# Soft mixture-of-experts in a perceiver block: combine gates turned as plain exponentials and normalised on VectorE as they leave PSUM

## What is computed

```
logits = (x @ phi_w.T + phi_b).reshape(t, z, n=64 experts, p=32 slots)
D = softmax(logits, axis=slots)        # dispatch weights
C = softmax(logits, axis=experts)      # combine weights (the gates)
X_tilde = einsum('tznp,tzd->npd', D, x)
X_tilde = clip(X_tilde, -33000, 65000)
X_tilde = tanh((X_tilde - mean) * rsqrt(var + 1e-5))
Y_tilde = einsum('npd,ndH->npH', X_tilde, expert_w) + expert_b
out = x + einsum('tznp,npH->tzH', C, Y_tilde)
```

## Time and profile before

| | us |
|---|---|
| median of 3 runs | 644.53 (641.23 to 645.74) |
| the profiled execution's own time | 640.95 |
| its span in the profile | 639.2 |

### The profile page before, as it was taken

The page is one execution under the profiler, slowest core; times in us unless marked ns, Lnnn a source line. Parts: engine busy times, 40 slices in busy tenths (PEclk is TensorE's granted clock), DMA queues, the critical chain, the costliest instruction groups (busy, mean ns, idle before and its releaser), DMA issues. The chain is left out here.

```text
span 639.2 us, 10389 instructions
## 1 busy us (share of the span) xinstructions
PE 583.5 (91%) x3740; PEld 469.4 (73%) x3740; DVE 406.8 (64%) x798; ACT 337.5 (53%) x988; POOL 255.0 (40%) x209
## 2 busy tenths in 40 slices
PE   5998999999999999998797789899999993699998
PEld 4887999899989999987565566455556882577787
DVE  3756565756665667644777586788889986733100
ACT  2545454434544446752787585259889953343210
POOL 1353153313241325124479464223455867643000
PEclk9999999999999999999999699999999998799999
DMA  7223121212110220067057500400000925359000
GB/s 267 71 99 116 35 67 67 84 49 84 67 67 34 71 88 26 3 193 203 1 155 199 175 1 1 133 1 0 1 1 19 180 67 197 102 179 300 31 26 25
DMA packets 39688, 55.62 MB, mean 87 GB/s; under 512 B 3923, under 2 KB 34515, under 8 KB 38870
## 3 DMA queue, kind: packets, MB, share of 16 engines
q1 hardware_dynamic: 39638, 54.97, 28.4%
HBM read 47.60 MB, written 7.35 MB: 86 GB/s over the span
## 5 line engine op out<-in xcount | busy, mean ns | idle before, releaser
L382 POOL TENSOR_TENSOR ctx_lo<-front,ctx_hi 128x1024 fp32r<-128x1024 f32 x32 | 76.4, 2389 | 155.7 <-DVE ctx_hi L824 135.4
L490 PE MATMUL ps<-ctx_hi,pT_hi 128*128 128x256 f32 x256 | 75.2, 294 | 1.0 <-DVE pT_lo L839 1.0
L839 DVE TENSOR_TENSOR pT_lo<-ps,pT_hi 128x512 fp32r<-128x512 f32 x64 | 41.2, 685 | 50.0 <-ACT pT_hi L694 50.0
L492 PE MATMUL ps<-ctx_hi,pT_lo 128*128 128x256 f32 x256 | 72.5, 283 | 0.0
L491 PE MATMUL ps<-ctx_lo,pT_hi 128*128 128x256 f32 x256 | 72.4, 283 | 0.0
L671 ACT CAST ctxT_hi<-ps 128x512 fp32r<-128x512 f32 x64 | 34.5, 593 | 62.6 <-PE ps L447 62.5
L1749 PE MATMUL ps<-front,turned 128*128 128x512 f32 x128 | 60.2, 591 | 0.0
L1797 PE MATMUL ps<-front,comb 128*128 128x256 f32 x256 | 57.8, 381 | 0.0
L1692 POOL TENSOR_TENSOR disp<-disp,dinv 128x512 f32<-128x512 f32 x32 | 33.5, 1048 | 57.0 <-DVE dinv L1964 56.9
L694 ACT CAST pT_hi<-ps 128x512 fp32r<-128x512 f32 x64 | 34.3, 589 | 36.8 <-PE ps L472 36.8
L1797 PEld LDWEIGHTS ps<-front,comb 128*128 128x128 f32 x256 | 47.6, 190 | 7.6 <-issue 1.6
(11 more groups left out here) (236 smaller groups left out, 1397.3 us busy)
## 6 DMA issues: line engine op xcount, KB each, us to landing
front<-in_ctx_dram SPq DMA_DIRECT2D x32, 512.0 KB, 3.3
back<-in_L_ffn_expert_w_dram SPq DMA_DIRECT2D x11, 1024.0 KB, 5.2
turned<-in_L_ffn_expert_w_dram SPq DMA_DIRECT2D x5, 1024.0 KB, 5.5
disp<-qk_parts_dram SPq DMA_DIRECT2D x4, 768.0 KB, 6.0
disp<-in_L_ffn_phi_w_dram SPq DMA_DIRECT2D x1, 2048.0 KB, 11.3
front<-in_L_ffn_expert_b_dram SPq DMA_DIRECT2D x4, 512.0 KB, 10.9
qk_parts_dram<-scores SPq DMA_DIRECT2D x4, 384.0 KB, 5.2
front<-qk_parts_dram SPq DMA_DIRECT2D x2, 768.0 KB, 5.3
```

The lines of the kernel that those rows point to most:

```text
L382: nc.gpsimd.tensor_tensor(ctx_lo[:, cols], ctx_in_sb[:, c % SLOTS, :], ctx_hi[:, cols].bitcast(F32), ALU.subtract).then_inc(split_g, 1)
L490: nc.tensor.matmul(pO[q][:, 0:D], pT_hi[:, c % 2, q, cols], hi, start=c == 0 and j == 0, stop=False)
L492: last = nc.tensor.matmul(pO[q][:, 0:D], pT_lo[:, c % 2, q, cols], hi, start=False, stop=c == NCH - 1 and j == J - 1)
L839: nc.vector.tensor_tensor(pT_lo[:, c % 2, q, :], probs_banks(c, alone)[q][:], pT_hi[:, c % 2, q, :].bitcast(F32), ALU.subtract).then_inc(p ...
```

## The change

The gates are no longer normalised on POOL. PE turns the plain exponentials, and the turned piece is multiplied by turned reciprocals when it is taken out of PSUM. The reciprocals of row c are written four times side by side (`cinv` is now 128 tokens x 4 experts x 32 slots), so that turned (one more 128 x 128 product in `experts(s)`, into free columns of the PSUM bank of that step's output) they are a tile of 128 slots x 128 tokens which fits each slot tile. DVE copies that tile into `cinvT`, which lies in a part of `disp` that is free by then, after `outputs(s)`. `inverse_at` says at which step: rows 0 to 3 at steps 0 to 3, rows 4 to 7 at steps 7 to 10. `combine_out` moves from ACT to DVE and becomes a multiply. POOL's 32 pieces of division go, and its subtraction is cut into pieces of 512 with the scales between the halves. The shift -mean * rstd moves from DVE to ACT as three small activations a pair: negate rstd, then multiply each of the two means. The last 8 `slot_exp` move in front of `combine_exp(4)`. DVE's list is reordered.

```diff
         srstd = sb("srstd", [P, PAIRS, 2])
+        sneg = sb("sneg", [P, PAIRS, 2])
         snmr = sb("snmr", [P, PAIRS, 2])
...
         csum = sb("csum3", [P, TT, NS])
-        cinv = sb("cinv", [P, TT, NS])
+        cinv = sb("cinv", [P, 4, EPT, NS])
+        cinvT = disp[:, 1, 0:TT * P].rearrange("p (t k) -> p t k", t=TT)
...
             return (s // 2 - 2, s % 2 * 2, s % 2 * 2 + 2) if 12 <= s else None
+        def inverse_at(s):
+            return {0: 0, 1: 1, 2: 2, 3: 3, 7: 4, 8: 5, 9: 6, 10: 7}.get(s)
...
-            def subtract_combine(c):
+            def subtract_combine(c, first=0, end=LB):
                 pool.wait_ge(cneg_v, c + 1)
-                row = by_expert(comb[:, c, :])
-                nc.gpsimd.tensor_tensor(row, row, cneg[:, c, :].unsqueeze(1).broadcast_to([P, NE, NS]), ALU.add).then_inc(csub_g, 1)
-            def divide_combine(c, k):
-                pool.wait_ge(cinv_v, c + 1)
-                part = by_expert(comb[:, c, k * 512:(k + 1) * 512])
-                nc.gpsimd.tensor_tensor(part, part, cinv[:, c, :].unsqueeze(1).broadcast_to([P, EB, NS]),
-                                        ALU.mult).then_inc(cmul_g, 1)
-            def divide_all(c):
-                for k in range(LB):
-                    divide_combine(c, k)
+                for k in range(first, end):
+                    part = by_expert(comb[:, c, k * 512:(k + 1) * 512])
+                    nc.gpsimd.tensor_tensor(part, part, cneg[:, c, :].unsqueeze(1).broadcast_to([P, EB, NS]),
+                                            ALU.add).then_inc(csub_g, 1)
...
                 divide_dispatch(u)
-                if u in (17, 18, 19, 20, 25, 26, 27, 28):
-                    divide_combine(u // 8 - 2, (u - 1) % 4)
                 if u == NU - 2:
...
             subtract_combine(SLOTWISE + 1)
-            input_scale(0)
-            input_scale(1)
-            input_scale(2)
-            divide_all(2)
+            for q in range(3):
+                input_scale(q)
+            subtract_combine(SLOTWISE + 2, 0, 2)
             input_scale(3)
-            subtract_combine(SLOTWISE + 2)
+            subtract_combine(SLOTWISE + 2, 2, LB)
             input_scale(4)
-            divide_all(3)
+            subtract_combine(SLOTWISE + 3, 0, 2)
             input_scale(5)
-            subtract_combine(SLOTWISE + 3)
+            subtract_combine(SLOTWISE + 3, 2, LB)
             input_scale(6)
             input_scale(7)
-            for c in range(SLOTWISE, TT):
-                divide_all(c)
...
             def transpose_combine(c, first, end):
+                if c < SLOTWISE:
+                    pe.wait_ge(cslot_a, NS * (c + 1))
+                else:
+                    pe.wait_ge(cexp_a, c - SLOTWISE + 1)
                 for k in range(first, end):
-                    pe.wait_ge(cmul_g, LB * c + k + 1)
-                    at_least(pe, cT_a, LB * c + k - 1)
+                    at_least(pe, cT_v, LB * c + k - 1)
                     for j in range(4):
...
                 at_least(pe, mixed_v, s - 1)
+                c = inverse_at(s)
+                if s >= 2 and inverse_at(s - 2) is not None:
+                    pe.wait_ge(cinvT_v, inverse_at(s - 2) + 1)
+                if c is not None:
+                    pe.wait_ge(cinv_v, c + 1)
+                    nc.tensor.transpose(psE[s % 2][:, HID:HID + P], cinv[:, c % 4, :, :].rearrange("p n s -> p (n s)"), ident[:])
                 for n in range(EPT):
...
                         pe.wait_ge(clip_v, 14 if t < 2 else ST)
-                        pe.wait_ge(cT_a, LB * (t + 1))
+                        pe.wait_ge(cT_v, LB * (t + 1))
                     if end > first:
...
             for t in range(TT // 2, TT):
-                pe.wait_ge(cT_a, LB * (t + 1))
+                pe.wait_ge(cT_v, LB * (t + 1))
                 mix(t, 0, ST).then_inc(y_mm, 1)
...
             def combine_exp(c):
-                act.wait_ge(csub_g, c - SLOTWISE + 1)
+                act.wait_ge(csub_g, LB * (c - SLOTWISE + 1))
                 nc.scalar.activation(comb[:, c, :], comb[:, c, :], ACT.Exp).then_inc(cexp_a, 1)
-            def combine_out(c, first, end):
-                for k in range(first, end):
-                    act.wait_ge(cT_mm, LB * c + k + 1)
-                    nc.scalar.copy(comb[:, c, k * 512:(k + 1) * 512], psC[k % 2][:]).then_inc(cT_a, 1)
...
                 q = s // 2
-                act.wait_ge(snmr_v, q + 1)
+                if s % 2 == 0:
+                    act.wait_ge(srstd_g, q + 1)
+                    nc.scalar.activation(sneg[:, q, :], srstd[:, q, :], ACT.Identity, scale=-1.0).then_inc(sneg_a, 1)
+                    act.wait_ge(sneg_a, q + 1)
+                    for k in (0, 1):
+                        nc.scalar.activation(snmr[:, q, k:k + 1], smv[:, q, k, 0:1], ACT.Identity, scale=sneg[:, q, k:k + 1]).then_inc(snmr_a, 1)
+                act.wait_ge(snmr_a, s + 1)
                 at_least(act, xT_mm, s - 1)
...
-            while slot < SLOTWISE * NS - 8:
+            while slot < SLOTWISE * NS:
                 slot_exp(slot)
...
                     input_tanh(s + 1)
-                if s < 2:
-                    for _ in range(4):
-                        slot_exp(slot)
-                        slot += 1
                 act.wait_ge(xT_mm, s + 1)
...
                 nc.scalar.copy(xhT[:, s % 2, :, :].rearrange("p c s -> p (c s)"), psT[s % 2][:, 0:DH * P]).then_inc(xT_a, 1)
-                if turned_at(s) is not None:
-                    combine_out(*turned_at(s))
                 if s in (4, 8):
                     combine_exp(SLOTWISE + 1 + s // 4)
-            combine_out(TT - 2, 0, LB)
-            combine_out(TT - 1, 0, LB)
         @block.vector
...
                     dve.wait_ge(csum_v, c - SLOTWISE + 1)
-                nc.vector.reciprocal(cinv[:, c, :], csum[:, c, :]).then_inc(cinv_v, 1)
+                at_least(dve, cinvT_v, c - 3)
+                nc.vector.reciprocal(cinv[:, c % 4, :, :], csum[:, c, :].unsqueeze(1).broadcast_to([P, EPT, NS])).then_inc(cinv_v, 1)
...
-            def input_shift(q):
-                dve.wait_ge(srstd_g, q + 1)
-                nc.vector.scalar_tensor_tensor(out=snmr[:, q, :], in0=smv[:, q, :, 0], scalar=-1.0,
-                                               in1=srstd[:, q, :], op0=ALU.mult, op1=ALU.mult).then_inc(snmr_v, 1)
+            def combine_out(c, first, end):
+                dve.wait_ge(cinvT_v, c + 1)
+                for k in range(first, end):
+                    dve.wait_ge(cT_mm, LB * c + k + 1)
+                    part = comb[:, c, k * 512:(k + 1) * 512].rearrange("p (j t) -> p j t", j=4)
+                    nc.vector.tensor_tensor(part, psC[k % 2][:].rearrange("p (j t) -> p j t", j=4),
+                                            cinvT[:, c, :].unsqueeze(1).broadcast_to([P, 4, P]), ALU.mult).then_inc(cT_v, 1)
...
                 nc.vector.tensor_tensor(mixed[:, s, :], psE[s % 2][:, 0:HID], mixed[:, s, :], ALU.add).then_inc(mixed_v, 1)
+                c = inverse_at(s)
+                if c is not None:
+                    nc.vector.tensor_copy(cinvT[:, c, :], psE[s % 2][:, HID:HID + P]).then_inc(cinvT_v, 1)
...
             combine_max(TT - 1)
-            combine_invert(2)
-            input_statistics(0)
-            input_statistics(1)
-            input_shift(0)
-            input_statistics(2)
-            input_shift(1)
-            input_statistics(3)
-            input_shift(2)
-            input_statistics(4)
-            input_shift(3)
+            for q in range(6):
+                input_statistics(q)
             dve.wait_ge(eb_in, 16 * EPT)
...
                 outputs(s)
-                if s < 3:
-                    input_statistics(s + 5)
-                if s == 1:
-                    combine_invert(3)
-                if s < 4:
-                    input_shift(s + 4)
-                if s in (1, 3, 6, 9):
-                    combine_invert(SLOTWISE + s // 3)
+                if s < 2:
+                    input_statistics(s + 6)
+                    combine_invert(s + 2)
+                if s in (2, 3, 5, 7):
+                    combine_invert(SLOTWISE + (2, 3, 5, 7).index(s))
+                if s + 1 < ST and turned_at(s + 1) is not None:
+                    combine_out(*turned_at(s + 1))
+            combine_out(TT - 2, 0, LB)
+            combine_out(TT - 1, 0, LB)
             for t in range(TT):
```

More of the change, by code:

```diff
@@ L1621, in soft_moe @@
         dmax_v, dsub_v, dexp_a, dsum_v, dinv_v, dmul_g = (sem(n) for n in ("dmax_v", "dsub_v", "dexp_a", "dsum_v", "dinv_v", "dmul_g"))
-        cneg_v, cslot_a, csub_g, cexp_a, csum_v, cinv_v, cmul_g = (sem(n) for n in (
-            "cneg_v", "cslot_a", "csub_g", "cexp_a", "csum3_v", "cinv_v", "cmul_g"))
-        cT_mm, cT_a = sem("cT_mm"), sem("cT_a")
-        xs_mm, clip_v, sst_v, smv_v, sve_v, srstd_g, snmr_v, tanh_a = (sem(n) for n in (
```

(6 more changed lines are left out.)

## The result

| | before | changed | ratio, 95% interval |
|---|---|---|---|
| first comparison, 5 runs each, median us | 644.53 | 648.89 | 1.0073 (1.0040 to 1.0106) |
| second comparison, 9 and 20 runs | 646.08 | 649.24 | 1.0048 (1.0022 to 1.0074) |
| profiled execution, its time | 640.95 | 647.65 | |
| its span | 639.2 | 645.9 | |

The change costs 3 to 4.4 us. I had forecast 1.1 us less and a range that ends at 647.5, so both the sign and the range were missed.

What follows compares the result with a forecast made beforehand. PE's 15.1 us of waits for DVE's `outputs` were taken as the limit behind the first stage; -4.2 + 2.7 + 0.2 = -1.3, taken as -1.1, put the median at 643.4 us from 644.5, range 639.5 to 647.5.

Steps and rivals of the forecast that it cites:

- The stall and where it goes: Second stage: PE's 12.5 us stop for `outputs` becomes stops of 7.65 and 4.3 us, waiting for DVE's multiply.
- The first stage: Division pieces leave POOL's list ahead of a dispatch product: PE wins 0.45 us, bounds 0 and 0.96.
- near 544: Time in us at which PE should turn gate row 1, which it did at 549.88 before.
- The reciprocal: DVE's reciprocal of 128 elements a row instead of 32: 0.47 us start to start, 0.96 with the dearest row.
- the rival: Clock falls in the second stop too, PE waiting for row 2's first multiply: 2.3 us, time 645.7; chance 0.30.
- The first fall: Low clock from the 7.65 us stop: 5.3 us of work at the lower level behind 540.35, costing 2.7 us.
- The sum: Whole kernel: -4.2 + 2.7 + 0.2 = -1.3 us with the second stop's clock unharmed, taken as -1.1.
- The multiply itself: DVE's multiply of 128 x 512 out of PSUM: 0.58 us, upper bound 0.69.
- The four late turnings of reciprocals: Late extra turning products on PE: 0.2 us lost; each of the eight extra products takes 0.13.
- The third rival: DVE dearer in reciprocals, multiplies and port waits: +6 us with the second clock fall, middle +3, 647.5; chance 0.13.

Runs made afterwards that it cites:

- The narrow variant: The changed kernel with VectorE reciprocals of 32 elements a row and the fourfold widening by a copy on ScalarE: 647.65 us, ratio 1.0027 to the kernel before.
- The shift alone: The kernel before with only the shift moved from VectorE to ScalarE as three small activations: 631.61 us, ratio 0.9806.
- the sums late: The changed kernel with sums of gate rows 4 to 7 moved behind outputs 7 to 10, their reciprocals turned two steps later: 636.13 us, ratio 0.9878.
- stops filled: The changed kernel with 60 and 32 idle turning products in TensorE's two stops: 645.53 us, ratio 1.0010 to the kernel before.
- second stop filled: The changed kernel with 34 idle turning products in TensorE's second stop alone, at gate row 2: ratio 1.0038 to the kernel before.
- both edits: The changed kernel with sums of gate rows 4 to 7 behind outputs 7 to 10, and 32-element reciprocals widened on ScalarE: 636.76 us, ratio 0.9867.
- sums spaced with the cut: The kernel before with shift on ScalarE, sums behind outputs 4, 5, 7 and 9, and GpSimd's subtraction in 512-column pieces: 630.49 us, ratio 0.9765.
- the sums spaced: The kernel before with the shift on ScalarE and sums of gate rows 4 to 7 behind outputs 4, 5, 7 and 9: 630.19 us, ratio 0.9785.

## Why the prediction was wrong

*The stall and where it goes: right.* The 12.5 us stop went, TensorE was found waiting for the multiply in two places, and these lasted 8.1 and 4.6 us where I had 7.65 and 4.3. The first stage gained 0.4 for 0.45. Row 1 was turned 1.8 us later than I wrote, in the changed profile's own time moved by its later start (548.94 - 3.15 = 545.8, for "near 544").

*The reciprocal: mis-sized.* The step "I take 0.47, start to start" failed. It is 0.87 (543.24 to 544.11), and the line's durations are

```profile
L1972 DVE RECIPROCAL cinv<-csum x8: 895/947/954, 458.8 to 578.8; 128x128 f32<-128x128 f32 x8
```

That is just inside the upper bound that I had written down, 0.96, and I had drawn the slope through the cheaper of two readings, least to least, across a difference of 42 ns. From 253 ns for 16 elements to 947 for 128 it is 6.2 ns an element. The narrow variant takes 0.60 off each reciprocal, which is worth 1.5 to 1.9 us ahead of the second stop's end. The forecast had 0.20 of the 0.60, so what it lacked is two thirds of that, 1.0 to 1.3 us. The Trainium skill's page VectorE: DVE Perf Modes, section First, the fixed hardware budget, with its repeat count of 8, pointed the right way here, and I set it aside too quickly: the estimate from it was 0.80 us for the 96 added elements, measured are 0.60 (947 - 349 ns). The measurement lies between my reading and the page's.

*The clock: the rival happened.* I gave 0.30 to a second fall of the clock in a stop of 4.3 us and 0.45 to none. This is the larger step that failed: the forecast put the second stop's low clock at nothing. It fell in both changed profiles, in the stop's last microsecond, and cost 2.4 to 2.8 us, for the 2.3 of the rival. The first fall cost 1.4 and not 2.7. The low stretch lasted 3.5 to 4.0 us behind that stop (544.79 to just before 549 in the first profile), and I had taken 5.3. Part of it is also paced by VectorE: the eight products took 1.97 us there against 1.25 at the upper level, not twice as long. The Trainium skill's page TensorE: Matmul & The Clock Gate, section HAM oscillation, warns that waits that recur pay each time, and the trace agrees: two low stretches for two stops, of 8.1 and 4.6 us.

*The sum.* My forecast of -1.1, corrected by +1.0 to +1.3 for the reciprocals, +2.4 to +2.8 for the second fall and -1.3 for the first, becomes +1.0 to +1.7, where the two stages show 3.2 to 3.6. Some 1.5 to 2.6 are missing. A part of them can be read off TensorE's timelines. A turned row at the upper clock takes 2.60 us (567.22 to 569.82) where it took 2.38 before (561.62 to 564.00), because its second half waits 0.42 us for the multiply and takes 1.25, and waited 0.33 for ScalarE's copy and took 1.12. In rows 1, 3, 6 and 7 that makes 0.9. The multiply itself, 0.60 from start to start, is hardly dearer than the 0.58 that I had. The four late turnings of reciprocals cost 0.11 each, 0.4 for my 0.2. The rest, some 0.4 to 1.5 us, stays open, and I tested none of it alone. The third rival held dear reciprocals and multiplies together with the second fall, and its middle of 647.5 was the nearest of my four times to the 648.9 measured.

*The range.* The errors that I had bounded one by one (dear reciprocals, two falls of the clock) came together. I had set them into a rival of 0.13 with its middle at the range's end. The second fall doesn't hang on the reciprocals: with narrow ones the stop was 3.98 us, shorter than the 4.3 of the forecast, and the clock fell behind it all the same.

*What I did not see.* I never priced the two halves of the change apart. The shift alone is worth 12.6 us, and the sum over the whole hid that the rest of the change costs 16 in the order as written, and 2.2 with the sums late.

## What to carry to other kernels

When work moves onto an engine whose list is in order, write down what stands ahead of the first instruction that the critical engine waits for; here sums of 3.6 us, for gate rows that are turned ten steps later or more, made a loss of 0.5 to 0.7% out of a gain of 1.2%. Price the parts of a change one by one before adding them up, since one part can pay for the whole while another gives it back. A stop of TensorE costs its length and can cost a stretch of low clock behind it, and the latter counts nearly in full where TensorE, not the engine it waits for, sets the pace. Before a difference of 1 or 2 us between two profiles is laid on an edit, compare the granted clock in their windows: in two of the pairs here it made most of the difference.

## What the runs showed of the hardware that I had not expected

The granted clock falls in some profiles and not in others at the same place of the same instructions. At the first stage's start TensorE waits 2.12 us for the normalised tokens. In the profile with late sums, which differs from the changed kernel only behind this place, the clock fell there (window, columns as above):

```profile
413.00:418.00 5.00, 5.00 (x16) 2.87 (x17) 1.30 (x3) 0.28 (x1) 1.05 (x1) 0.66 0.02 3
```

In both profiles of the changed kernel it did not, and in the second of them TensorE got through 24 instructions in six microseconds instead of 16 in five:

```profile
412.00:418.00 6.00, 5.94 (x24) 3.73 (x25) 3.47 (x8) 1.19 (x3) 1.66 (x2) 1.00 0.01 3
```

Of the 12 profiles of this study the clock fell there in six (late sums, shift only, stops filled, second stop filled, both edits, sums spaced with the cut), whose first stages took 119.0 to 119.6 us, and not in the other six, with 117.3 to 117.8. So it is worth about 1.7 us. Three kernels that have the changed kernel's instructions up to this place (late sums, stops filled, second stop filled) showed it, and neither profile of the changed one did. No kernel has a profile of each kind, so whether chance decides, or something in each program, stays open. Together with the first logit, which started anywhere from 399.5 to 403.5 us, it means that the spans of two single profiles may differ by some 5 us over code that is the same.

A VectorE instruction of 128 x 2 elements, all in SBUF, can wait for the GpSimd work beside it: the small add took 4.47 us beside a subtraction of a whole row and 1.20 at the same place beside pieces of 512 columns, where its usual time is 0.17. But a piece's end doesn't always free it. In the variant with the cut another of these adds took 3.48 us beside four division pieces back to back, here on the timeline of VectorE and GpSimd:

```profile
535.86 4.99 POOL L1706 TENSOR_TENSOR comb<-comb,cinv 128x512 f32<-128x512 f32 x4
...
537.42 3.48 DVE L2021 TENSOR_SCALAR sve<-smv 128x2 f32<-128x2 f32 x1
```

It ended at 540.90, with the last of the four at 540.85. I have no run that tells why one add got in between two pieces and the other did not. VectorE instructions that read PSUM, and its sums and reciprocals, showed no such wait. With the sums spaced, `outputs` took 0.42 us beside division pieces, a sum 3.75 beside divisions and a subtraction, and a reciprocal 0.35 beside a subtraction, which is what they take elsewhere (0.36 to 0.42, 3.56 to 3.80 and 0.35).
